# Three edits to a long-convolution and adapter kernel: inverses of a group's first two pairs one step sooner, the turn of the normalised tile behind the last transform, three tensors kept on chip

## The reference

```python
def layer_1(x):                          # x is layernorm of the input
    proj = (x @ in_proj_w + in_proj_b).reshape(B, L, C, 3)
    v = proj[..., 0]
    v = depthwise_conv3(v) + short_b
    h = gelu(gelu(pos @ fw1 + fb1) @ fw2 + fb2)
    coefs = (h @ fw3 + fb3).reshape(L, C, 2)
    for i in range(2):                   # only i = 1 reaches the output
        conv = irfft(rfft(v, 2 * L) * rfft(coefs[:, :, i], 2 * L))[:L]
        output = proj[..., i + 1] * conv
    return output @ out_w + out_b

def layer_2(x):                          # x is layernorm again
    out = einsum('k,kod,bsd->bso', weights, W[ids], x)   # 8 of 32 adapters, mixed
    return out + einsum('k,ko->o', weights, b[ids])

x = x + layer_1(layernorm(x)); x = x + layer_2(layernorm(x))
```

## Time and profile before

| | us |
|---|---|
| median of 3 runs (2350.34 to 2353.32) | 2351.52 |
| the profiled execution, its own time | 2352.14 |
| its span, first to last instruction | 2350.2 |
| PE busy | 2297.2 (98%) |
| DVE busy | 1528.0 (65%) |
| POOL busy | 931.4 (40%) |
| ACT busy | 845.2 (36%) |

### The profile page before, as it was taken

One profiled execution on the slowest core, in us unless ns is written; L12 is line 12 of the kernel. 1 busy time (PEld: TensorE's weight loads), 2 busy tenths in 40 slices (PEclk: granted clock), 3 DMA queues, 4 the chain that ended last, 5 costly groups with the idle time before them and its releaser, 6 DMA issues.

```text
span 2350.2 us, 39731 instructions
## 1 busy us (share of the span) xinstructions
PE 2297.2 (98%) x12804; PEld 1618.0 (69%) x12804; DVE 1528.0 (65%) x2180; ACT 845.2 (36%) x1155; POOL 931.4 (40%) x1183
## 2 busy tenths in 40 slices
PE   8899999999999999999999969999999999999998
PEld 2577777777777777544444437777777777777776
DVE  7644444444443434477777758888888888888886
ACT  5444444444444444444444422222222222222222
POOL 2222222222222222000000027777777777777774
PEclk9899999999999999999999989999999999999999
DMA  9645454555455556699999988766565666665653
GB/s 295 203 147 181 144 166 147 183 173 185 132 176 165 160 192 252 233 344 357 358 362 356 352 313 261 211 177 181 174 179 176 179 178 179 177 180 172 183 173 99
DMA packets 180301, 496.60 MB, mean 211 GB/s; under 512 B 19203, under 2 KB 19524, under 8 KB 159116
## 3 DMA queue, kind: packets, MB, share of 16 engines
q1 hardware_dynamic: 150540, 395.10, 52.7%
q10 hardware_dynamic: 29696, 100.68, 11.8%
HBM read 276.24 MB, written 219.43 MB: 211 GB/s over the span
## 4 chain that ended last, share of the span: by engine, by line
PE 53%; DVE 2%; issue 2%; DMA 1%; POOL 0%; SPq 0%; DVEq 0%; ACT 0%; POOLq 0%
PE m_psW L1056 7%; PE m_psA L1039 6%; PE b_psF L183 6%; PE b_psF L184 5%; PE b_psC L1361 5%; PE b_psF L185 5%; PE b_psO L184 5%; PE b_psO L185 5%; PE b_psO L183 5%; PE b_psT L1392 2%; PE b_psP L1375 2%; DVE m_m L1128 2%; DMA b_fin<-wide_out 1%; DMA spec<-wide_out 0%; DMA b_edge_b<-edge_f 0%
## 5 line engine op out<-in xcount | busy, mean ns | idle before, releaser
L1128 DVE TENSOR_TENSOR m_m<-m_psA,m_spec 128x1024 f32<-128x1024 f32 x256 | 295.6, 1217 | 110.6 <-PE m_psA L1039 108.9
L771 POOL TENSOR_TENSOR vl<-v,vh 128x512 fp32r<-128x512 f32 x128 | 165.2, 1291 | 390.1 <-ACT vh L729 390.1
L1323 ACT ACTIVATE b_zh<-b_psT 128x512 fp32r<-128x512 f32 x128 | 76.4, 597 | 634.5 <-PE b_psT L1392 634.5
L1056 PE MATMUL m_psW<-m_m,mats 64*64 64x512 f32 x2048 | 251.7, 589 | 0.0
L1039 PE MATMUL m_psA<-m_xin,mats 64*64 64x512 f32 x1536 | 208.6, 599 | 10.4 <-DVE m_m L1128 5.7
L872 DVE TENSOR_TENSOR gto<-psG,bgr 128x512 f32<-128x512 f32 x128 | 87.5, 684 | 195.3 <-PE psG L185 195.1
L183 PE MATMUL psV<-wvh,nth 128*128 128x512 f32 x512 | 213.7, 417 | 0.6 <-DVE ntl L853 0.6
L183 PE MATMUL b_psO<-woh,b_oh 128*128 128x512 f32 x512 | 210.7, 411 | 0.0
L183 PE MATMUL b_psF<-wfh,b_zh 128*128 128x512 f32 x512 | 207.9, 406 | 2.8 <-DVE b_zl L1462 2.8
L729 ACT ACTIVATE vh<-v 128x512 fp32r<-128x512 f32 x128 | 80.9, 632 | 341.0 <-DVE v L865 341.0
L184 PE MATMUL b_psF<-wfl,b_zh 128*128 128x512 f32 x512 | 201.4, 393 | 0.0
(11 more groups left out here) (138 smaller groups left out, 4661.9 us busy)
## 6 DMA issues: line engine op xcount, KB each, us to landing
spec<-wide_out SPq DMA_DIRECT2D x64, 1024.0 KB, 9.1
spec<-wide_out ACTq DMA_DIRECT2D x64, 1024.0 KB, 9.5
b_fin<-spec SPq DMA_DIRECT2D x126, 512.0 KB, 4.6
m_xin<-spec SPq DMA_DIRECT2D x30, 2048.0 KB, 11.8
xg<-in_L_attn_x_dram SPq DMA_DIRECT2D x64, 512.0 KB, 6.2
gate_d<-gto SPq DMA_DIRECT2D x32, 1024.0 KB, 4.0
b_gin<-gate_d SPq DMA_DIRECT2D x128, 256.0 KB, 3.6
b_xin<-in_L_attn_x_dram SPq DMA_DIRECT2D x256, 128.0 KB, 3.2
```

Source lines behind the costliest of these rows:

```text
L771: pool.tensor_tensor(vl[:, t % 2], v[:, t % 2], vh[:, t % 2].bitcast(F32), ALU.subtract).then_inc(v_lo, 1)
L1056: mm = pe.matmul(psW[pair % 2][half[slot], q, :], ws[slot][half[q]], m[half[q], pair % RM, part, slot, :], start=part == 0, stop=part == 1)
L1128: dve.tensor_tensor(m[:, (k - 2) % RM, part], psA[k % RA][:], spec[:, par, part], ALU.mult).then_inc(m_done, 1)
```

## The change

- In `middle` the inverses of pairs 0 and 1 get lag 1, that of pair 2 keeps lag 2, that of pair 3 lag 3, on PE and for ACT's copies.
- In `back` the turn of z for odd tiles stands directly behind `conv_pair`; for even tiles it stays behind `adapt`.
- The mixed adapter, its bias and `b_s4` live on chip through the whole program, at the other end of the memory. `b_s4` is loaded in the front's first batch; the stores to `ad_mix` and `ad_bias` and their loads are gone; `ad_sum` serves as `res` in `back`, and as the buffer `wide` in `prep`. out_w is loaded to the buffer of x in `middle` instead of to `b_res`, so the first loads of x wait for `low`. `gto` now shares its place with tiles of `middle`, so DVE's first product waits for the stores of the gates.

The diff, cut to its core:

```diff
-    ad_mix = nc.dram_tensor("ad_mix", [P, CT, C], F32, kind="Internal").ap()
-    ad_bias = nc.dram_tensor("ad_bias", [P, C], F32, kind="Internal").ap()
...
-            wide = sb("wide", [P, L])
+            wide = kept["ad_sum"][:].rearrange("p k c -> p (k c)")
...
-            ad_sum = sb("ad_sum", [P, CT, C])
...
-            adb_sum = sb("adb_sum", [P, C])
+            ad_sum, adb_sum = kept["ad_sum"], kept["adb_sum"]
+            gto = sb("gto", [P, 2, SUB, C])
...
+                def load_last_transform(b, t):
...
+                    if isinstance(b, int) and b == 0 and t == 2:
+                        sp.dma_start(kept["s4"][:], consts["s4"]).then_inc(kept["s4_in"], 16)
...
-                def store_mix(b, t):
...
-                    if isinstance(b, int) and b == B - 1 and t == MIX:
-                        sp.wait_ge(ad_used, MIX * B)
-                        sp.dma_start(ad_mix, ad_sum[:]).then_inc(ad_stored, 16)
-                        sp.dma_start(ad_bias, adb_sum[:]).then_inc(ad_stored, 16)
...
-            wraw = bc["res"]
+            wraw = bc["xin"]
...
-                sp.dma_start(bc["s4"][:], consts["s4"]).then_inc(bc["s4_in"], 16)
...
-                sp.dma_start(bc["bfr"][:], ad_bias).then_inc(bc["rows_in"], 16)
                 sp.dma_start(bc["ident"][:], consts["ident"]).then_inc(bc["ident_in"], 16)
+                sp.wait_ge(low, 1)
                 for t in range(EARLY):
...
-                sp.wait_ge(low, 1)
-                sp.dma_start(wraw[:], ad_mix).then_inc(bc["ad_in"], 16)
...
-                def inverse_early(i, s):
-                    if 2 <= s % GS < GS - 1:
+                def inverse_first(i, s):
+                    if 2 <= s % GS < GS - 2:
+                        inverse(i, s)
...
+                def inverse_third(i, s):
+                    if s % GS == GS - 2:
                         inverse(i, s)
...
-                pipelined(pe, GROUPS // 2, S, [(forward, 0), (inverse_early, 2), (inverse_last, 3)])
+                pipelined(pe, GROUPS // 2, S, [(forward, 0), (inverse_first, 1), (inverse_third, 2), (inverse_last, 3)])
...
-                pipelined(act, GROUPS // 2, S, [(spectrum, 0), (out_early, 2), (out_last, 3), (w_high, 3)])
+                pipelined(act, GROUPS // 2, S, [(spectrum, 0), (out_first, 1), (out_third, 2), (out_last, 3), (w_high, 3)])
...
+                    if at_first(i, s) and k == 2:
+                        for slot in range(2):
+                            dve.wait_ge(mc["g_stored"][slot], 16 * B * Q // 2)
...
-            edge_a, fin, gin, xin, res = (bc[k] for k in ("edge_a", "fin", "gin", "xin", "res"))
+            s4, res, bfr = kept["s4"], kept["ad_sum"], kept["adb_sum"]
...
-                        if d == 0:
-                            pe.wait_ge(bc["ad_in"], 16)
...
+                def turn_z_behind_conv(b, t):
+                    if t % 2:
+                        turn_z(b, t)
...
+                def turn_z_behind_adapt(b, t):
+                    if t % 2 == 0:
+                        turn_z(b, t)
...
-                pipelined(pe, B, T, [(conv_pair, 0), (turn_w, 0), (adapt, 5), (turn_z, 4), (turn_o, 1), (project, 2)])
+                pipelined(pe, B, T, [(conv_pair, 0), (turn_w, 0), (turn_z_behind_conv, 4), (adapt, 5), (turn_z_behind_adapt, 4), (turn_o, 1), (project, 2)])
...
+        kept = {
+            "ad_sum": hold_right("ad_sum", [P, CT, C], until=ctx), "adb_sum": hold_right("adb_sum", [P, C], until=ctx),
+            "s4": hold_right("b_s4", [P, N2, N1], until=ctx), "s4_in": sem("b_s4_in"),
+        }
```

More of the change, by code:

```diff
@@ L554, in _, with front @@
                     dve.bn_aggr(fc["mv"][:, 0, i], fc["stats"][:, 0, i]).then_inc(fc["mv_done"], 1)
-    def front(fc, mc):
+    def front(fc, mc, kept):
         with ExitStack() as st:
@@ L691, in load_first_groups @@
                     sp.dma_start(mc["xin"][:, g, 0:B - 1], spec1[rows, 0:B - 1]).then_inc(mc["early_in"][g], 16)
[L693 to L701 removed]
+                pipelined(sp, B, T, [(load_x, 0), (save_v0, 5), (load_adapter, 6), (store_gate, 8), (store, 9), (load_first_groups, 11), (load_last_transform, 11)])
                 sp.wait_ge(v0_out, 16 * B)
@@ L1130, in _, with back @@
                 pipelined(dve, GROUPS // 2, S, [(product, 0)])
-    def back(bc):
+    def back(bc, kept):
         with ExitStack() as st:
@@ L1138, in ps @@
                 return st.enter_context(nc.psum_tensor(name, [P, C], F32))
-            s4, woh, wol, wfh, wfl, v0_first, bor, bfr, ident = (
-                bc[k] for k in ("s4", "woh", "wol", "wfh", "wfl", "v0_first", "bor", "bfr", "ident"))
-            edge_a, fin, gin, xin, res = (bc[k] for k in ("edge_a", "fin", "gin", "xin", "res"))
+            s4, res, bfr = kept["s4"], kept["ad_sum"], kept["adb_sum"]
+            woh, wol, wfh, wfl, v0_first, bor, ident = (
+                bc[k] for k in ("woh", "wol", "wfh", "wfl", "v0_first", "bor", "ident"))
+            edge_a, fin, gin, xin = (bc[k] for k in ("edge_a", "fin", "gin", "xin"))
             corr, corr_step, corr_done = (bc[k] for k in ("corr", "corr_step", "corr_done"))
@@ L1492, in hyena_adapter_kernel, with hold_right @@
         both = ExitStack()
-        def hold_right(name, shape, dt=F32):
-            return both.enter_context(nc.sbuf_tensor(name, shape, dt, side="right"))
-        hold_right("right_pad", [P, 8])
+        def hold_right(name, shape, dt=F32, until=both):
+            return until.enter_context(nc.sbuf_tensor(name, shape, dt, side="right"))
+        hold_right("right_pad", [P, 8], until=ctx)
+        kept = {
+            "ad_sum": hold_right("ad_sum", [P, CT, C], until=ctx), "adb_sum": hold_right("adb_sum", [P, C], until=ctx),
+            "s4": hold_right("b_s4", [P, N2, N1], until=ctx), "s4_in": sem("b_s4_in"),
+        }
         mc = {
@@ L1505, in hyena_adapter_kernel @@
         }
-        prep(fc, mc)
-        front(fc, mc)
+        prep(fc, mc, kept)
+        front(fc, mc, kept)
     with ExitStack() as st:
@@ L1512, in hyena_adapter_kernel @@
         bc = {
-            "s4": hold("b_s4", [P, N2, N1]),
             "woh": hold("woh", [P, CT, C], F32R), "wol": hold("wol", [P, CT, C], F32R),
             "wfh": hold("wfh", [P, CT, C], F32R), "wfl": hold("wfl", [P, CT, C], F32R),
-            "v0_first": hold("b_v0_first", [P, C]), "bor": hold("bor", [P, C]), "bfr": hold("bfr", [P, C]),
+            "v0_first": hold("b_v0_first", [P, C]), "bor": hold("bor", [P, C]),
             "ident": hold("b_ident", [P, P]),
@@ L1519, in hyena_adapter_kernel @@
             "corr": hold("b_corr", [P, 2, C]), "corr_step": sem("b_corr_step"), "corr_done": sem("b_corr_done"),
-            "edge_a": hold("b_edge_a", [P, EARLY, 2, C]), "res": hold("b_res", [P, D, C]),
+            "edge_a": hold("b_edge_a", [P, EARLY, 2, C]),
             "spec_stored": [[sem(f"m_stored{k}{i}") for i in range(2)] for k in range(2)],
-            "s4_in": sem("b_s4_in"), "v0_in": sem("b_v0_in"), "rows_in": sem("b_rows_in"), "ident_in": sem("b_ident_in"),
-            "ad_in": sem("b_ad_in"), "edge_in": [sem(f"b_edge_in{i}") for i in range(T // 2)],
+            "v0_in": sem("b_v0_in"), "rows_in": sem("b_rows_in"), "ident_in": sem("b_ident_in"),
+            "edge_in": [sem(f"b_edge_in{i}") for i in range(T // 2)],
             "f_in": [sem(f"b_f_in{i}") for i in range(2)], "tail_in": [sem(f"b_tail_in{i}") for i in range(EARLY)], "g_in": [sem(f"b_g_in{i}") for i in range(2)],
@@ L1528, in hyena_adapter_kernel @@
         both.close()
-        back(bc)
+        back(bc, kept)
 _INS = ['L0_attn_x', 'L0_attn_in_proj_w', 'L0_attn_in_proj_b', 'L0_attn_short_w', 'L0_attn_short_b', 'L0_attn_fw1',
```

17 lines of the change are left out of this document (9 added, 8 removed).

## The result

The changed kernel takes 2337.38 us (median of 4 runs, 2335.71 to 2339.51) beside 2351.93 for the kernel before: ratio 0.9937, 95% interval 0.9925 to 0.9948, 14.8 us less. 2344.0 was forecast with a range from 2337 to 2351.5; the sign is right, the gain is twice the forecast, and the time lies 0.4 us inside the range. The profiled execution lasted 2337.9 us at a span of 2336.1, so 14.1 us less than the span before.

A forecast was written before the change was run, and what follows sets the result against it. PE was taken to bound the kernel nearly everywhere, except short waits in the middle's groups and the handover. Terms 0 - 0.5 + 3 - 8.5 - 1.5 = -7.5 us gave 2344.0 us beside 2351.52, range 2337 to 2351.5.

The forecast's parts named there:

- Order of the inverses, 0 and -0.5: Middle: PE's wait only moves one block later, 0 over 30 inner groups; first group and end give -0.5 us.
- 3.44 us again, against the same 3.91: Middle: PE's work between forward blocks sharing a PSUM tile, against the tile's round trip; 0.38 to 0.47 us still lost.
- Loads, +3: Middle: large loads, issued later, lose their spare; 0.1 us on each of 29 groups, +3 us, bounds 0 and 29.
- The two I let cancel: Middle: one store issued beside the load, the store before given more time to drain; taken as no net effect.
- The late load: Rival, middle: first forward block waits for its load; full form 2360 us, chance 0.07; mild form 2351, chance 0.18.
- Kept on chip, -8.5: Handover: fewer loads, edge rows issued at 1378.7 instead of 1387.21; -8.5 us, bounds -5.8 and -11.5.
- the chain behind them is unchanged: Handover: waits from the edge rows to the turn of z stay as long, so their 8.5 us carries through.
- Chain and bytes: Handover: gain set by the last store's chain, -8.5 us, or, as rival, by bytes, 5.8 to 6.6; rival's chance 0.17.
- Turn of z, -1.5: Back: turn behind conv changes each of 64 pairs by -0.07 to +0.02 us; -1.5 us, bounds -4.5 and +1.7.
- as many as before: Back: turns between full-rate blocks and changes between matmul kinds stay the same in number.
- The wait does go: Rival, middle: DVE's products begin sooner, so the next group's first forward block finds its tile free; -13 us, 2331, chance 0.08.
- The ceiling of 358 GB/s: Middle and handover: a core's memory share would make a group's transfers take 12.45 us, the present period, and the handover -6.6.

The follow-up runs named there:

- order_only: The kernel before with only the new order of the inverses; 2348.17 us, ratio 0.9981 to the kernel before.
- halves: The changed kernel with the middle's inverses cut in two halves and reordered on PE, ACT's copies reordered to suit; 2332.32 us, ratio 0.9909 to the kernel before.
- halves_split: The changed kernel with inverses cut in halves and reordered, and each group's large load cut in two; 2321.33 us, ratio 0.9866 to the kernel before.
- the split alone: The changed kernel with each group's large load cut in two, its own order on PE kept; 2330.19 us, ratio 0.9906 to the kernel before.
- f4_wait: The changed kernel with an added wait, without effect, on DVE ahead of the third pair's first product; 2339.05 us, ratio 0.9938 to the kernel before.

## Why the prediction was right in sign and short in size

That the time lies in the range is in part luck. The order and the loads together came out 6.3 us better than forecast and the turn of z 5.1; the kept tensors came out 3.3 worse, and 2.2 us more in the first groups took another part back.

- *Order of the inverses, 0 and -0.5.* The wait moved from F4 to F0 as worked out. The step that failed is "3.44 us again, against the same 3.91": the 1.41 us from F2 to DVE were carried over to F4, where the way is 1.21, with one instruction less behind PE's signal. The sum is 3.72, the wait 0.28, and the middle gained 3.8 us (order_only's profile).
- *Loads, +3.* Wrong: F0 waited for its load in three of the first groups, 1.3 us in all, and in none from 1040 on. "The two I let cancel" is the step: the moved stores did not cancel out. No longer two at a time beside the load, they took it from 11.8 to 10.0 us. The spare grew from 1.4 to 1.7 instead of shrinking to 0.1. The Trainium skill ("DMA: Bandwidth & Descriptors", "Issuing engines are not separate DMA queues") says that transfers of both issuers interleave on the same engines; the three landing times above agree. The late load did come, in halves.
- *Kept on chip, -8.5.* 5.2 us in the handover of the changed kernel; alone 7.3, of which 5.7 are left at the next conv. The first conv was expected at 1374 and came at 1375.44, the edge rows at 1378.7 and at 1378.31. But the reason given, the last store, is wrong: they wait for the first conv, through SP's queue, and the middle's own gain is in these times too. And "the chain behind them is unchanged" failed: they landed 8.1 us behind their issue (1386.39), before 6.3. Chain and bytes are one thing here, since the conv waits for transfers. Not foreseen: kept tensors make the old order's pair 0.02 us longer, and its period in the middle 0.05 shorter.
- *Turn of z, -1.5.* Mis-sized, 6.6 in the changed kernel's back, outside its bound of 4.5. The adapter's 2.83 and the turn's lower value came true: a steady pair is 0.09 shorter. From the third conv to the last that gives 4.7 us, since two early pairs take 15.2. And one thing was left out, worth 1.8: from the last conv to the end it is 35.6 us instead of 37.4, since there the last z is turned before the adapter of the tile ahead of it. The count was wrong too: changes between matmul kinds are not "as many as before" but seven a pair instead of six. It is who stands next to conv that pays, not their number.
- *The rivals.* None came as written. "The wait does go" had the right seed, DVE beginning sooner behind F4, and a third of the wait went. The ceiling of 358 GB/s that the Trainium skill gives ("DMA: Bandwidth & Descriptors", "Where 436 GB/s comes from") is not one here: halves_split moved 373 GB/s for 301 us. The Trainium skill's "HBM Reference" ("Specifications (TRN2)") gives more to a core that streams alone, which fits; what the other core of the pair did, no run here shows.

## What to carry to other kernels

A round trip is measured at the block where the wait will stand, not at the one where it stands: what the waiting engine's queue has to do between the signal and the work can differ, by 0.1 us an instruction here. A moved store changes how long the load beside it takes, so compare how far apart they are issued before taking a landing time over. When a transfer is made to come sooner, look through the whole queue of its issuer for what else it waits for. And when one wait goes, name the next and have its cure ready: halves alone gave 6.6 us over the changed kernel, the split alone 7.3, both together 16.7.

## What the runs showed of the chip that I had not expected

PE stood idle for 0.9 to 4.3 us near the start of the middle's loop, put down to no releaser, in all twelve kernels with one large load, and not at all in the two with the load in two. Waits of PE from 967 to 1040, in f4_wait:

```profile
PE m_psA L1029 <- issue: 3.1, 1, 3.1
PE m_psW L1046 <- issue: 1.2, 1, 1.2
```

Why is open. So is this: behind each change to `mm3` it takes 3 to 11 matmuls at 224 to 236 ns until the steady 227 is reached, and how many differs between kernels whose code on PE is the same. That makes the 14.81 and 14.83 us of one order, and part of the 14.78 and 14.72 of the other.
